# Constant matrix products in TensorE's waits, written into the PSUM bank of the job that follows

## The reference

```
x += tanh(g_xattn[0]) * attention(norm(x), ctx, mask)    # A: 16 heads of 8, 77 keys
x += tanh(g_ffn[0])   * top-2 mixture(norm(x))           # B: 8 experts 128->512->128, capacity 320, and a shared one
x += tanh(g_xattn[1]) * attention(norm(x), ctx)          # C: as A, without mask
x += tanh(g_ffn[1])   * mixture-of-heads attention(...)  # D: self-attention, 8 heads of 16
```

## Time and profile before

| | |
|---|---|
| median of 3 runs | 329.53 us (329.13 to 333.83) |
| the profiled execution's own time | 330.81 us |
| its span, first to last instruction | 329.0 us |
| TensorE busy | 245.6 us (75%) |
| VectorE / ScalarE / GpSimd busy | 120.3 / 99.8 / 75.5 us |
| mean granted clock | 0.825 |

### The profile page before, as it was taken

The page is one execution under the profiler, slowest core; times in us unless marked ns, Lnnn a source line. Parts: engine busy times, 40 slices in busy tenths (PEclk is TensorE's granted clock), DMA queues, the critical chain, the costliest instruction groups (busy, mean ns, idle before and its releaser), DMA issues.

```text
span 329.0 us, 3845 instructions
## 1 busy us (share of the span) xinstructions
PE 245.6 (75%) x1461; PEld 133.8 (41%) x1461; DVE 120.3 (37%) x376; ACT 99.8 (30%) x153; POOL 75.5 (23%) x94
## 2 busy tenths in 40 slices
PE   1899799788648813999980367787786788979874
PEld 0333343233433712787860132232232425537542
DVE  2834333303548100011222885343042861380211
ACT  2210244155206101744320012361555012440540
POOL 2800320001122771054461250000026260000000
PEclk9999999679958985999997555796599855896995
DMA  7999100000000116000015000000000000000000
GB/s 250 402 398 205 55 0 0 2 0 0 1 2 8 57 48 173 2 28 22 29 35 143 0 0 0 2 0 0 1 2 0 0 0 2 0 0 2 2 34 32
DMA packets 13819, 15.92 MB, mean 48 GB/s; under 512 B 1303, under 2 KB 10906, under 8 KB 13802
## 3 DMA queue, kind: packets, MB, share of 16 engines
q1 hardware_dynamic: 12272, 12.86, 12.9%
q0 software_dynamic: 1152, 2.05, 1.9%
q10 hardware_dynamic: 378, 0.78, 0.7%
HBM read 10.74 MB, written 5.26 MB: 49 GB/s over the span
## 4 chain that ended last, share of the span: by engine, by line
PE 41%; issue 32%; DVE 11%; ACT 6%; DMA 4%; SPq 3%; POOL 2%; ACTq 0%; DVEq 0%; POOLq 0%
PE wk L729 6%; PE ts L696 5%; PE wk L537 5%; PE ts L579 3%; SPq L353 3%; ACT pr L924 3%; PE wk L605 3%; PE wk L620 3%; DVE nmx L1061 3%; PE ts L569 2%; PE wk L498 2%; DVE xn L1048 2%; PE wk L541 2%; DMA x<-in_x 2%; PE wk L711 1%
## 5 line engine op out<-in xcount | busy, mean ns | idle before, releaser
L1061 DVE TENSOR_REDUCE nmx<-wk 128x4 f32<-128x308 f32 (+1 forms) x94 | 46.1, 540 | 42.1 <-PE wk L541 36.2
L924 ACT ACTIVATE pr<-ts 77x1024 f32<-77x1024 f32 x32 | 30.9, 1015 | 36.4 <-PE ts L584 19.7
L390 POOL TENSOR_TENSOR rstd<-ve,half 128x4 f32<-128x4 f32 (+1 forms) x8 | 9.7, 1206 | 125.9 <-DVE ve L1043 125.9
L438 POOL DMA_INDIRECT y_d<-onT,dst_i x20 | 19.5, 973 | 30.3 <-DVE onT L1284 17.3
L488 PE MATMUL wk<-pk,xn 128*128 128x128 f32 x32 | 8.2, 404 | 22.6 <-DVE xn L1048 20.6
L537 PE MATMUL wk<-w,qT 32*128 32x512 f32 x60 | 20.7, 747 | 3.3 <-DVE nmx L1061 1.9
L729 PE MATMUL wk<-w,pr 128*128 128x128 f32 (+1 forms) x192 | 22.0, 278 | 0.0
L729 PEld LDWEIGHTS wk<-w,pr 128*128 128x128 f32 (+1 forms) x192 | 20.6, 173 | 2.8 <-issue 2.0
L984 ACT ACTIVATE pr<-ts,pk 128x320 f32<-128x320 f32 x32 | 16.6, 528 | 16.4 <-PE ts L696 16.2
L431 POOL DMA_INDIRECT xs_d<-xn,slot_i x16 | 15.8, 990 | 14.3 <-DVE slot_i L1240 9.7
L696 PE MATMUL ts<-pr,w 128*128 128x320 f32 x64 | 18.4, 433 | 0.0
(11 more groups left out here) (182 smaller groups left out, 370.9 us busy)
## 6 DMA issues: line engine op xcount, KB each, us to landing
w<-in_w SPq DMA_DIRECT2D x8, 512.0 KB, 11.6
xs_d<-fill SPq DMA_DIRECT2D x1, 1290.0 KB, 17.8
pr<-xs_d SPq DMA_DIRECT2D x5, 258.0 KB, 3.8
y_d<-fill SPq DMA_DIRECT2D x1, 1024.0 KB, 19.4
y<-y_d SPq DMA_DIRECT2D x4, 256.0 KB, 3.8
pk<-in_pk SPq DMA_DIRECT2D x1, 942.0 KB, 8.9
x<-in_x SPq DMA_DIRECT2D x2, 256.0 KB, 5.8
sw<-in_sw SPq DMA_DIRECT2D x2, 256.0 KB, 8.1
```

The costliest lines, as they stand in the source:

```text
L438: pool.indirect_dma_start(y_d, bass.IndirectOffsetOnAxis(ap=dst_i[:, i:i + 1], axis=0), ostage[:, i % 4, :], None, bounds_check=2 * NTOK - ...
L924: m = act.activation(prs[u][0:NK, r, 2 * i:2 * i + 2, :], ts[0:NK, 2 * i:2 * i + 2, :], ACT.Exp)
L1061: v.tensor_reduce(dst, src, AX.X, ALU.max, negate=True).then_inc(job_dve, 1)
```

## The change

A helper `keep_warm` issues a number of products of two constants: the weights are the 128 x 128 bf16 matrix of ones, the moving operand the first 512 columns of the bf16 constants. Nobody reads the result; it is written to the bank that the next job has just been given and will overwrite. The helper is called after the wait for the bank and before the wait for the job's data. The counts stand in the table `WARM_X` for `transposes_x` (92 in all), are 8 for each of the six `transposes_max`, and 40 ahead of the first group of `gathered`: 180 products in all.

```diff
+WARM_X = {("A", 0): 8, ("A", 1): 0, ("B", 0): 0, ("B", 1): 18, ("C", 0): 60, ("C", 1): 6, ("D", 0): 0, ("D", 1): 0}
...
+            def keep_warm(w, n):
+
+                for _ in range(n):
+                    pe.matmul(w, onesb, bpk[:, 0:S].bitcast(BF16), start=True, stop=True)
+
...
             def transposes_x(L, b):
                 w = bank("xT", L, b)
+                keep_warm(w, WARM_X[L, b])
                 for t in range(TB):
                     pe.wait_ge(xn_ready, TB * LN[L, b] + t + 1)
...
             def transposes_max(L, b):
-                w = bank("nT", L, b).bitcast(BF16)
+                w = bank("nT", L, b)
+                keep_warm(w, 8)
+                w = w.bitcast(BF16)
                 pe.wait_ge(nsp_ready, UNIT[L, b] + 1)
...
             def gathered(n):
                 w = bank("xg", n)
+                if n == 0:
+                    keep_warm(w, 40)
                 pe.wait_ge(xg_in[n], 16)
```

## The result

| | before | changed |
|---|---|---|
| median (range), 4 runs each | 331.68 us (329.13 to 339.06) | 310.46 us (308.85 to 310.73) |
| ratio, 95% interval | | 0.936 [0.925, 0.946] |
| profiled execution, span | 330.81, 329.0 us | 308.85, 307.0 us |
| mean granted clock | 0.825 | 0.922 |

The change is faster by 6.4%; the forecast was 306 us with a range of 299 to 317. Two more executions of the changed kernel, not in the table, took 307.07 and 313.98 us. Some executions are slower, at a lower granted clock; the medians and ranges include them, the ratios leave them out.

What follows compares the result with a forecast made beforehand. TensorE, slow after each wait, alternates with short chains on VectorE and ScalarE; a wait costs itself and the slow clock after it. Terms sum to 24.8 us, taking 330.81 us to 306 us, range 299 to 317.

Steps and rivals of the forecast that it cites:

- A 0: First wait: eight products make the transposes 2.4 us late but raise the clock early, speeding maxima and later work; minus 9.8 us.
- That rival: First 43 us slow for another reason than the clock: A 0 costs 2.4 us, total 318 us; chance 5%.
- The waits of 2.0 us: Eight products fit before the maxima's transposes, keeping the clock fast: A 1 minus 3.2, C 1 minus 4.0, D 1 minus 2.1 us.
- B 1: 18 products fit into 4.87 us; transposes lose 0.5 and logits 0.9 us; minus 1.4 us.
- The gather: 40 products take 8.8 us of an 11.2 us wait; half of 1.2 us on its transposes counted; minus 0.6 us.
- D 0: Eight products before the maxima's transposes start slow, 1.7 us late, then the clock rises; minus 1.6 us.
- C: 60 products give almost nothing, C 1's six come 2.6 us late but raise the clock: minus 2.1, second half minus 4.0 us.
- The tail: Last 10 us of the kernel: no products there, slow as before, no gain.
- no 0.50 between 20 and 100 us: Sign expected in the changed profile: the granted clock never at 0.50 between 20 and 100 us.
- the products that don't raise or hold the clock: Rival, all stages: each product takes 0.43 us wherever it stands, together +33.5 us, 364 us; chance 4%.
- the clock holds through the maxima of D: Rival, stage D: the clock stays up through its maxima, 5 us more gain, 301 us; chance 7%.
- On transposes: Rival: transposes don't count for the clock; gather and B 1's transposes give nothing, C's rise 1 us later; 308 us; 3%.

Runs made afterwards that it cites:

- the last kernel: The change without the gather's 40, with 20 products in B 1, 67 in C 0, 18 ahead of C 1's bank wait, more in D: 298.92 us, ratio 0.896.
- the change once more: The changed kernel, unaltered, rerun on the chip of three further kernels: 314.57 us (308.28 to 325.13), with the kernel before at 332.5 us.

## Why the prediction was right, point by point

The table sets the terms against the two profiles: a row is the start of the same instruction before and after, the shift, and what the shift grew by since the row above.

| up to | before | after | shift | grown by | predicted |
|---|---|---|---|---|---|
| A 1, transposes of the maxima | 61.02 | 49.70 | 11.3 | 11.3 | 9.8 |
| B 0, transposes | 84.47 | 69.85 | 14.6 | 3.3 | 3.2 |
| first scatter | 103.88 | 89.35 | 14.5 | -0.1 | 1.4 |
| C 0, transposes | 185.85 | 175.75 | 10.1 | -4.4 | 0.6 |
| C 0, second scores | 211.41 | 199.70 | 11.7 | 1.6 | 2.1 |
| D 0, transposes | 247.35 | 231.41 | 15.9 | 4.2 | 4.0 |
| D 1, transposes of the maxima | 296.32 | 277.93 | 18.4 | 2.5 | 1.6 |
| D, the step behind the 64 values | 303.11 | 281.86 | 21.2 | 2.9 | 2.1 |
| end | 328.99 | 307.04 | 21.9 | 0.7 | 0 |

**A 0** was right in its mechanism and too small. The page's 1.00 in the first 43 us is indeed not the clock; with eight products in front, every shape of this stage has its later time, and the two kernels with and without the eight show this alone (28.05 and 38.21 us for the transposes of the maxima). That rival is out. The transposes came 2.1 us late, as priced at 2.4, and this cost nothing. Up to the first exponentials, where the prediction ends this term, it gave 41.85 - 31.16 = 10.7 us, 0.9 more than priced, and 0.6 more followed before A 1's transposes. Most of the 0.9 is the first pair of maxima, which came at 17.38 and not 18.29 us. The prediction had VectorE busy until about 18 there, but its own row shows VectorE idle for 1.60 us before 18.29, waiting for slow products.

**The waits of 2.0 us** (A 1, C 1, D 1) are where nearly half of the gain is. Term by term they came to 3.3 + 4.2 + 2.9 = 10.4 us for a forecast of 9.3. Taking all six fills out cost more, about 17 us; in that profile the clock also falls in A 0 (29.3 us) and stays down to 206.8 us in C 0. The forecast has the reason: a wait costs a second time by the clock behind it, and there stand the scores that ScalarE waits for.

**B 1** gave nothing, not 1.4 us. The transposes took 1.10 us at a granted clock of 1.00, against 1.16 at 0.50: they follow the tiles of `xn` as these come, so the 0.5 us priced for them were never there. And after rests of 0.90 and 0.78 us with 1.1 us of work between them the clock fell at 81.8, just as the logits had begun; they took 1.63 us where 0.95 was assumed. With all but the first eight products the same two rests are there, but the clock fell only behind the logits, which took 1.03 us; the first scatter then came 18.5 us after B 0's transposes, against 19.5 in the change and 19.4 before. So some 0.9 us can be had here, when the clock happens to hold that long.

**The gather** is the term that was wrong: plus 4.4 us, not minus 0.6. The step that failed is "40 x 0.22 = 8.8 us of a wait of 11.2 us". The wait of 11.2 us was read from the recorded ends of TensorE's instructions. In that execution the result of the work in front of it was released only at 126.8 us, so that work behind it could count on 128.4 - 126.8 = 1.6 us, not 11.2. (How much TensorE did between 117.2 and 126.8 isn't shown; the clock fell at 121.4.) The products delayed the gather by 6.3 us and gave back 4.15 - 2.18 = 2.0 us from there to the first expert. The sign is visible in the trace of before, in VectorE's wait of 9.26 us for a bank that TensorE seemed to have left long ago, which the prediction did not look at. On chips without this standstill no effect of the 40 is shown (ratios 0.921 and 0.928 with and without them). And what was won there was lost again later: the kernel without the 40, on a chip without the standstill, reaches C's transposes 3.8 us before the first profile of the change (171.95 and 175.75) and ends at 306.6 against 307.0. The change itself does the same on such a chip (172.08 and 306.7), so the 3.8 us are those of the standstill and not of the 40 alone.

That leads to **D 0**, where the clock fell in the maxima, the eight products ran slow and came 257.91 - 256.36 = 1.6 us late, as forecast with 1.7 (256.36 is 272.30 less the shift of 15.94). When it rises again is a matter of luck: at 259.3 us in the change, and in two executions of the same kernel (the one without the 40) at 262.4 and at 254.2 us though their instructions stood within 1.1 us of each other until then. The windows over the same stretch of D 0's first scores, first on the last chip of this study and then on that of the first experiments (window, length, busy and count of TensorE, its weight loads, VectorE, ScalarE, GpSimd, clock, DMA share, GB/s):

```profile
254.00:257.00 3.00, 2.69 (x31) 2.23 (x32) 0.17 (x1) 0.81 (x2) 0.00 (x0) 0.96 0.00 0
```

```profile
254.00:257.00 3.00, 2.39 (x12) 2.01 (x11) 0.43 (x1) 0.00 (x0) 0.00 (x0) 0.50 0.00 0
```

One gets through 31 instructions, the other through 12, and the spans are 302.3 and 306.6 us. So the 3.8 us won before C were given back here: the work was that much ahead, and the clock rose 3.1 us later (262.4 and 259.3). A forecast of single microseconds can't be had in this stretch.

**C** was right in its mechanism: nothing from the 60 products at their own transposes, 2.6 us late for the six of C 1 and at least as much back, 1.6 us in all where 2.1 was priced, and 4.2 us for 4.0 in the second half.

**The tail** was put at nothing and gave 0.7 us, since the clock fell later there, at 300.2.

The sum: minus 22.0 us against minus 24.8, and the error is the gather's 5.0, B 1's 1.5 and 0.5 in the first half of C, against 4.2 us that the others gave beyond their price. That the sum came within 2.8 us is in part luck: the misses of 7.0 and 4.2 us have opposite signs. Of the signs named beforehand one failed, "no 0.50 between 20 and 100 us": the clock was down from 81.8 to 88.6. Of the rivals, the products that don't raise or hold the clock are excluded by A 0, where it is up at 13.5 us with them and at 38.1 without, and by the 60 in C, (175.75 - 1.86 - 160.77) / 60 = 0.22 us each. That the clock holds through the maxima of D came true in none of the three profiles of the change; in two of them it fell in the wait of 1.65 us, in the third it was down from 232.1 us, with two short rises. It takes products in that wait, as the last kernel shows, and is then worth 3.5 us up to the transposes of the maxima.

On transposes the Trainium skill says, in "TensorE: Matmul & The Clock Gate", section "Part 4: PE-mode transpose", that they don't bring the full clock, as they don't count as activity. The experiment with 16 f32 transposes in the place of the products speaks against it for this type: 0.60 us for the next four, and 27.42 us for the transposes of the maxima. It is one execution. In the kernel without the 40 on the last chip, too, nothing but f32 transposes was on TensorE from 113.11 to 117.8 us before the clock rose at 117.7. No run here tried bf16 transposes.

## What to carry to other kernels

Where TensorE waits a couple of microseconds in front of work that another engine is waiting for, eight products of constants in the wait cost nothing if the clock is up when they begin, and the six such waits here were worth more than they are long, 17 us for 12.0. Where the clock had already fallen, as in D 0, the eight came 1.6 us late. Look for the steps that take twice their usual time right behind a wait, not for the longest wait. Put them ahead of the wait for the bank if that comes last, into PSUM that is free then, and let them end as close to the data as they can: a rest of 1.03 us in C 0 did no harm in the last kernel, while two of 0.90 and 0.78 us in B 1 did in the change. Before counting on an idle stretch of TensorE, look at when the engine that consumes its last result was released; here that was up to ten microseconds after the recorded end.

## What the runs showed of the hardware

- In six of the fourteen profiles (the first ones of before and of the change, and the four that begin with the change once more) VectorE was released 23.0 to 23.2 us after GpSimd's first scatter, though TensorE's records of that work end 8 to 10 us earlier; in the eight profiles of the two other chips it was 12.65 us. Kernels with 0, with 7 and with 40 products in the gather are among the eight, kernels with 0 and with 40 among the six: within these it goes with the chip or the session, and not with the kernel. It falls into the time of GpSimd's scatters. What holds TensorE up, fetching of its instructions or something else, was not tried.
- 16 f32 transposes of a constant raised the clock as eight products of 512 columns did (up at 11.1 us in one execution, against 11.6 to 13.9 in eleven).
- Before the first change of the clock in the records the profile shows 1.00, though the instructions of the first 43 us take their 1.2 GHz times.
- The clock fell with rests of under 2 us: within one of 1.65 us in the maxima of D, where TensorE had been busy without a pause from 239.2 to 244.4, and behind two of 0.90 and 0.78 us with 1.1 us of work between them in B 1. And it stayed at 0.50 through the 8.4 us of nearly unbroken work behind the one in D (246.06 to 254.5), mostly f32 products of 32 rows; it was up at 259.3, 1.2 us after the eight bf16 products of 128 rows.
